# Scores of an attention kernel: six half-row matmuls per head pair become four full-row matmuls over stacked high and low parts

## The reference

```python
xn = layernorm(x)
q  = heads(cq @ Wu_q) + heads(rope(cq @ Wq_r))      # cq  = xn @ Wd_q
k  = heads(ckv @ Wu_k) + heads(rope(xn @ Wk_r))     # ckv = xn @ Wd_kv
v  = heads(ckv @ Wu_v)
x  = x + layernorm(softmax(q k^T / sqrt(1040)) v @ Wo)
h  = gelu(layernorm(x) @ W1[7])
x  = x + layernorm((h @ W2[7]) * router_prob[7])
```

## Time and profile before

| | us |
|---|---|
| median of 2 runs (7258.16 to 7260.33) | 7259.24 |
| profiled execution | 7265.72 |
| its span, slowest core | 7264.1 |
| spans of the 8 cores | 7222.0 to 7264.1 |
| TensorE busy | 5700.7 (78%) |
| VectorE busy | 4018.6 (55%) |
| ScalarE busy | 2148.1 (30%) |
| chain of work that ended last, TensorE's share | 73% |

### The profile page before, as it was taken

One profiled execution on the slowest core, in us unless ns is written; L12 is line 12 of the kernel. 1 busy time (PEld: TensorE's weight loads), 2 busy tenths in 40 slices (PEclk: granted clock), 3 DMA queues, 4 the chain that ended last, 5 costly groups with the idle time before them and its releaser, 6 DMA issues.

```text
span 7264.1 us, 94919 instructions; the slowest of 8 cores (7222.0 to 7264.1 us)
## 1 busy us (share of the span) xinstructions
PE 5700.7 (78%) x26128; PEld 2435.2 (34%) x26128; DVE 4018.6 (55%) x7572; ACT 2148.1 (30%) x3157; POOL 189.0 (3%) x446
## 2 busy tenths in 40 slices
PE   3888888858788888888888888884546898888982
PEld 1333333323333333333333333331223343333430
DVE  3444444434388888888888888881223333333323
ACT  1111222111244444444444444442221011110113
POOL 1000000000000000000000000000000000000000
PEclk9888889879889988998898889886767999999996
DMA  4111111131111121111211121112101111111012
GB/s 110 47 47 47 52 52 52 50 80 37 50 50 51 51 59 52 52 51 52 59 51 51 48 64 51 51 48 62 35 32 38 25 28 35 35 35 33 22 34 90
DMA packets 480103, 357.82 MB, mean 49 GB/s; under 512 B 106863, under 2 KB 436591, under 8 KB 479612
## 3 DMA queue, kind: packets, MB, share of 16 engines
q1 hardware_dynamic: 445532, 316.05, 15.1%
q0 software_dynamic: 34080, 35.71, 3.0%
HBM read 294.73 MB, written 75.76 MB: 51 GB/s over the span
## 4 chain that ended last, share of the span: by engine, by line
PE 73%; DVE 11%; DMA 7%; issue 4%; ACT 4%; SPq 1%; DVEq 0%; ACTq 0%; POOL 0%; POOLq 0%
PE pall L288 42%; PE pall L863 18%; PE pall L900 9%; PE pall L905 4%; DVE sq_scr L943 3%; DMA w1h_sb<-w 2%; DMA kt_sb<-kT_hbm 1%; ACT sq_scr L303 1%; ACT sq_scr L300 1%; DVE xnTh_t L446 1%; ACT xn L432 1%; DVE sq_scr L954 0%; DVE ol_t L962 0%; DVEq L88 0%; DVE w1l_sb L1152 0%
## 5 line engine op out<-in xcount | busy, mean ns | idle before, releaser
L921 ACT ACTIVATE pt<-pall,negM 128x512 f32<-128x512 f32 x2048 | 1403.9, 687 | 1473.1 <-DVE ptl L930 687.2
L930 DVE TENSOR_TENSOR ptl<-pt,pth 128x512 bf16<-128x512 f32 x2048 | 1418.4, 693 | 219.4 <-DVE pth L926 8.3
L863 PE MATMUL pall<-pth,vt_sb 128*65 128x512 bf16 x4096 | 1330.4, 387 | 0.0
L926 DVE CAST pth<-pt 128x512 bf16<-128x512 f32 x2048 | 860.7, 420 | 107.1 <-ACT pt L921 98.4
L905 PE MATMUL pall<-qt_sb,kt_sb 64*128 64x512 bf16 x3072 | 857.2, 389 | 2.1 <-ACT pt L921 1.6
L900 PE MATMUL pall<-qt_sb,kt_sb 64*128 64x512 bf16 x3072 | 786.2, 391 | 81.5 <-DMA kt_sb<-kT_hbm 56.9
L863 PE MATMUL pall<-ptl,vt_sb 128*65 128x512 bf16 x2048 | 787.3, 384 | 4.3 <-DVE ptl L930 4.3
L863 PEld LDWEIGHTS pall<-pth,vt_sb 128*65 128x65 bf16 x4096 | 460.2, 112 | 598.6 <-issue 235.1
L288 PE MATMUL pall<-xn2Th_sb,w1h_sb 128*128 128x512 bf16 x1024 | 403.0, 394 | 255.3 <-DVE w1l_sb L1152 255.3
L1206 DVE TENSOR_TENSOR y_acc<-y_acc,pall 128x512 f32<-128x512 f32 x512 | 351.8, 687 | 280.8 <-PE pall L288 275.8
L1236 ACT ACTIVATE ao_t<-pall,b_col 128x512 f32<-128x512 f32 x128 | 88.0, 687 | 1396.4 <-PE pall L288 1270.6
(11 more groups left out here) (235 smaller groups left out, 6531.2 us busy)
## 6 DMA issues: line engine op xcount, KB each, us to landing
vt_sb<-v_hbm SPq DMA_DIRECT2D x512, 130.0 KB, 2.5
kt_sb<-kT_hbm SPq DMA_DIRECT2D x512, 128.0 KB, 2.4
xt<-xv SPq DMA_DIRECT2D x48, 512.0 KB, 4.1
wscr<-w SPq DMA_DIRECT2D x128, 128.0 KB, 2.3
wscr<-w SPq DMA_DIRECT2D x32, 512.0 KB, 4.4
v_hbm<-vh_t SPq DMA_DIRECT2D x32, 260.0 KB, 2.1
v_hbm<-vl_t SPq DMA_DIRECT2D x32, 260.0 KB, 2.1
xnT_hbm<-xnTh_t SPq DMA_DIRECT2D x64, 128.0 KB, 1.9
```

What stands on the lines that cost most here:

```text
L863: e.matmul(PB(hh)[0:65, 0:512], vf(), pf(), start=(kcp == 0 and pi == 0), stop=(kcp == 31 and pi == 2)), deps=dd)
L921: tex = p.do("scalar", lambda e, sbb=sbb, s32=s32: e.activation(pt32[:, 512 * s32:512 * s32 + 512], PB(sbb)[:, 0:512], AF.Exp, bias=negM[: ...
L926: thv = p.do("vector", lambda e, s=s, s32=s32: e.tensor_copy(pth[:, 512 * s:512 * s + 512], pt32[:, 512 * s32:512 * s32 + 512]), deps=[tex ...
L930: tlv = p.do("vector", lambda e, s=s, s32=s32: e.tensor_tensor(ptl[:, 512 * s:512 * s + 512], pt32[:, 512 * s32:512 * s32 + 512], pth[:, 5 ...
```

## The change

The high and low parts of a head are stacked on the partitions, so that one matmul contracts over 128 rows instead of 64. For Q, `qt_sb` holds for each head its high part on partitions 0 to 63 and its low part on 64 to 127. For K, the left half of `kt_sb` has [high; low] and the right half [low; high]. A first matmul gives hh + ll, a second lh + hl: so two full-row matmuls per head in place of three half-row ones, and the product ll is computed as well. `kt_sb` is twice as large, and `kT_hbm` has the layout [128, 32 chunks, 16 heads, 128], with the high part in rows 0 to 63.

```diff
-    kT_hbm = nc.dram_tensor("kT_hbm", [D, S // 128, 2, 128], BF16, kind="Internal").ap()
+    kT_hbm = nc.dram_tensor("kT_hbm", [128, S // 128, H, 128], BF16, kind="Internal").ap()
...
-            t1 = p.do("sync", lambda e, oc=oc, st=st: e.dma_start(
-                out=kT_hbm[128 * oc:128 * oc + 128, 4 * st:4 * st + 4, 0, :],
...
-            tsp = p.do("sync", lambda e, oc=oc, st=st: e.dma_start(
-                out=kT_hbm[128 * oc:128 * oc + 128, 4 * st:4 * st + 4, 1, :],
...
+            tsp = None
+            for ab in range(2):
+                h = 2 * oc + ab
+                t1 = p.do("sync", lambda e, h=h, ab=ab, oc=oc, st=st, tsp=tsp: e.dma_start(
+                    out=kT_hbm[0:64, 4 * st:4 * st + 4, h, :],
...
+                    deps=[th_, tl_] + ([tsp] if tsp is not None else []),
+                    dma=f"osp{oc}")
+                tsp = p.do("sync", lambda e, h=h, ab=ab, oc=oc, st=st, t1=t1: e.dma_start(
+                    out=kT_hbm[64:128, 4 * st:4 * st + 4, h, :],
...
+                    deps=[th_, tl_, t1], dma=f"osp{oc}")
...
-    kt_sb = [bsb(f"kt_sb{i}", [128, 512], BF16) for i in range(2)]
+    kt_sb = [bsb(f"kt_sb{i}", [128, 2 * 512], BF16) for i in range(2)]
...
-                qload.append(p.do("sync", lambda e, Q=Q, hp=hp, hl=hl: e.dma_start(
-                    out=qt_sb[:, 2048 * (2 * hp + hl):2048 * (2 * hp + hl) + 2048],
...
+        for h in range(4):
+            tqh = p.do("sync", lambda e, Q=Q, h=h: e.dma_start(
+                out=qt_sb[0:64, 2048 * h:2048 * h + 2048],
...
+            qload.append(p.do("sync", lambda e, Q=Q, h=h: e.dma_start(
+                out=qt_sb[64:128, 2048 * h:2048 * h + 2048],
...
+                deps=[LU.get("qt_sb"), tqh], dma=f"qld{h}"))
...
+                tk0 = p.do("sync", lambda e, Q=Q, kc=kc, bufi=bufi: e.dma_start(
+                    out=kt_sb[bufi][:, 0:512].rearrange("p (h k) -> p h k", k=128),
+                    in_=kT_hbm[:, kc, 4 * Q:4 * Q + 4, :]),
+                    deps=[LU.get(("kt", bufi))], dma=f"kt{bufi}")
+                tk1 = p.do("sync", lambda e, Q=Q, kc=kc, bufi=bufi: e.dma_start(
+                    out=kt_sb[bufi][0:64, 512:1024].rearrange("p (h k) -> p h k", k=128),
+                    in_=kT_hbm[64:128, kc, 4 * Q:4 * Q + 4, :]),
+                    deps=[LU.get(("kt", bufi)), tk0], dma=f"kt{bufi}")
                 tk = p.do("sync", lambda e, Q=Q, kc=kc, bufi=bufi: e.dma_start(
-                    out=kt_sb[bufi][:].rearrange("p (a hl k) -> p a hl k", a=2, k=128),
-                    in_=kT_hbm[256 * Q:256 * Q + 256, kc, :, :]
-                        .rearrange("(a p) hl k -> p a hl k", p=128)),
-                    deps=[LU.get(("kt", bufi))], dma=f"kt{bufi}")
+                    out=kt_sb[bufi][64:128, 512:1024].rearrange("p (h k) -> p h k", k=128),
+                    in_=kT_hbm[0:64, kc, 4 * Q:4 * Q + 4, :]),
+                    deps=[LU.get(("kt", bufi)), tk1], dma=f"kt{bufi}")
...
+                for hh in range(4):
+                    sb = 4 + hh
...
+                    t1 = p.do("tensor", lambda e, k1=k1, qs=qs, sb=sb: e.matmul(
+                        PB(sb)[:, 0:512], k1(), qs(), start=True, stop=False),
+                        deps=deps_s + bk.pre_write(sb))
+                    t2 = p.do("tensor", lambda e, k2=k2, qs=qs, sb=sb: e.matmul(
+                        PB(sb)[:, 0:512], k2(), qs(), start=False, stop=True),
+                        deps=deps_s)
```

More of the change, by code:

```diff
@@ L836, in build_program @@
         qload = []
-        for hp in range(2):
-            for hl in range(2):
-                qload.append(p.do("sync", lambda e, Q=Q, hp=hp, hl=hl: e.dma_start(
-                    out=qt_sb[:, 2048 * (2 * hp + hl):2048 * (2 * hp + hl) + 2048],
-                    in_=qT_hbm[256 * Q + 128 * hp:256 * Q + 128 * hp + 128, hl, :]),
-                    deps=[LU.get("qt_sb")], dma=f"qld{2 * hp + hl}"))
+        for h in range(4):
+            tqh = p.do("sync", lambda e, Q=Q, h=h: e.dma_start(
+                out=qt_sb[0:64, 2048 * h:2048 * h + 2048],
+                in_=qT_hbm[256 * Q + 64 * h:256 * Q + 64 * h + 64, 0, :]),
+                deps=[LU.get("qt_sb")], dma=f"qld{h}")
+            qload.append(p.do("sync", lambda e, Q=Q, h=h: e.dma_start(
+                out=qt_sb[64:128, 2048 * h:2048 * h + 2048],
+                in_=qT_hbm[256 * Q + 64 * h:256 * Q + 64 * h + 64, 1, :]),
+                deps=[LU.get("qt_sb"), tqh], dma=f"qld{h}"))
         for qt in range(4):
@@ L886, in build_program @@
                 sc_tok = [None] * 4
[L887 to L903, removed]
-                    for pi, (kf, qf) in enumerate([(kh, qh), (kh, ql), (kl, qh)]):
-                        tB = p.do("tensor", lambda e, kf=kf, qf=qf, sb1=sb1, pi=pi: e.matmul(
-                            PB(sb1)[:, 0:512], kf()[64:128, :], qf()[64:128, :],
-                            start=(pi == 0), stop=(pi == 2), tile_position=(64, 0)),
-                            deps=deps_s + (bk.pre_write(sb1) if pi == 0 else []))
-                    bk.wrote(sb0, tA)
-                    bk.wrote(sb1, tB)
-                    sc_tok[2 * hp] = tA
-                    sc_tok[2 * hp + 1] = tB
@@ new lines, in build_program @@
+                deps_s = [tk] + qload
+                for hh in range(4):
+                    sb = 4 + hh
+                    k1 = lambda bufi=bufi, hh=hh: kt_sb[bufi][:, 128 * hh:128 * hh + 128]
+                    k2 = lambda bufi=bufi, hh=hh: kt_sb[bufi][:, 512 + 128 * hh:
+                                                              512 + 128 * hh + 128]
+                    qs = lambda hh=hh, qt=qt: qt_sb[:, 2048 * hh + 512 * qt:
+                                                    2048 * hh + 512 * qt + 512]
+                    t1 = p.do("tensor", lambda e, k1=k1, qs=qs, sb=sb: e.matmul(
[4 more added lines that the diff above has]
+                        deps=deps_s)
+                    bk.wrote(sb, t2)
+                    sc_tok[hh] = t2
```

10 lines of the change are left out of this document (4 added, 6 removed).

## The result

The changed kernel is slower. The ratio of its time to that of the kernel before is 1.1923 (95% interval 1.1905 to 1.194), which on 7259.24 is 8655 us. The executions behind it lie between 8638.65 and 8663.67 us, and those of before between 7254.73 and 7260.33. In some executions of either kernel the cores of one die run at a lower granted clock and the time is some per cent longer (with them the median of all 11 is 8874.75), and comparisons here leave these out. The profiled execution took 8659.47.

A forecast was written before the change was run, and what follows sets the result against it. VectorE was taken to set the pace at 4.53 us per chunk, TensorE close behind. K loads 854, K stores 145 and Q loads 42 sum to 1041 us, added to 7259 for 8300; range 7950 to 8720.

The forecast's parts named there:

- upper bound of 7.1: Attention stage: us per chunk with all high bounds taken together; 6.4 was expected and 5.8 the low end.
- signs named ahead: Profile after: V issues 6 to 6.7 us apart, SP's K waits some 1600 us, VectorE idle up some 850, clock near 1.00.
- VectorE sets the pace before: Attention stage, kernel before: casts and subtractions fill 4.45 of 4.53 us per chunk; K load has about 1.3 us of slack.
- Score matmuls a draw: Attention scores: eight full-row matmuls need 8 slots, as now; gain 0, bounds a 0.45 us loss and 0.9 gain per chunk.
- K loads, 854 us: Attention stage: three chained loads make chunks 6.4 us for 4.56, over 464 intervals; bounds 575 and 1180.
- first term: Two-chunk loop: start of scores(k-1) to issue of V(k), 4.67 us, with TensorE's work unchanged.
- Rival A: Attention stage: TensorE's clock falls and half of the chunks run at the low level; 8900 us, chance 0.05.
- 0.66 for late landings: Two-chunk loop: 0.22 us added for each of three landings, as not all are at the median; 0.33 per chunk.
- K stores, 145 us: First stage: four stores with three waits per 128 columns delay V stores; 8 tiles x 18 us, bounds 88 and 225.
- Q loads, 42 us: Start of each of four head groups: eight loads with four waits, 11 us later each; bounds 25 and 60.
- Rival B: K loads: rows 128 KB apart in HBM make each landing 3.0 us; 7.7 per chunk, 8960 us, chance 0.10.
- Rival C: Whole kernel: waits are hidden, landings of 1.15 us each, VectorE still sets 4.53; 7260 us, chance 0.03.

The follow-up runs named there:

- the last pair: Changed kernel without SP's waits and kernel before, both with two casts on ScalarE and K ahead of V: ratios to kernel before 0.984 and 0.9868.
- e6_before_chain: Kernel before with its K load cut into three DMAs, each waiting for the landing of the one before: 8237.13 us, 6.66 per chunk.

## Why the prediction was right or wrong

The forecast was 8300 us, 1041 over before, in a range of 7950 to 8720; by the ratio it is 8655, 1396 over. The direction, the place and the mechanism of the waits are borne out. What is missing is the clock that falls in their idle time, and the size is 355 us short. That 8655 still lies in the range is luck: the chunks' 7.03 us is just under the upper bound of 7.1, which was built from slow and late landings, and the landings were neither; the clock filled that room. Of the signs named ahead, the K load as what TensorE waits for, the scores' 1.8 us and VectorE's busy time held. V issues came 7.03 us apart for 6 to 6.7, SP's waits were 1852 us for 1600, VectorE's idle time rose by 1161 for 850, the x loads went 26 us later for 18, and the granted clock in a block was 0.86 to 0.90 for 1.00.

- VectorE sets the pace before, with the K load 1.3 us from binding: right (casts moved: 4.56 to 4.41 per chunk; K load behind four issues: it binds).
- Score matmuls a draw: right, by the last pair: 1.76 us for eight full rows, 1.65 for twelve half ones. The Trainium skill (TensorEngine Tiling (Array Packing), Theoretical Speedup) gives up to 2x for a contraction of at most 64 rows, which for twelve half-row matmuls is six slots, an estimate of 1.3 us at 0.22; the trace agrees in the direction, and shows about 1.6x in this run (1.65 us) and 1.4x in the kernel before (1.82).
- K loads, 854 us: measured 1146. The step that failed is its first term, "start of scores(k-1) to issue of V(k) ... 4.67 ... TensorE's work is unchanged". The work is unchanged, the clock isn't: from 3827.19 to 3833.43 it took 6.24. Rival A was set aside because "the new gaps are short". The mean gap of 1.9 us was right (1.83), but once the clock had fallen it came as 3.4 in one chunk of two. I had the clock as a rival apart, with a chance of 0.05 and the price of half of all chunks; it was a part of the likeliest case, at 385 us. (The Trainium skill, TensorE: Matmul & The Clock Gate, HAM oscillation, describes a loop in which TensorE waits for a DMA in each turn, falls to the low clock in the wait and starts each turn at it. The forecast didn't weigh that section. The trace agrees in that the clock falls once per loop behind the long wait, 0.86 to 0.90 inside the blocks; it differs in that the first matmuls after the wait still have slots of 0.22 us.) The other terms were good: landings of 2.28, 2.15 and 2.13 for 2.4, 2.0 and 2.0, and 0.35. The 0.66 for late landings in a loop was too much: at a full clock the loops came to 12.4 on the mean, for 12.75. That error hid some of the first.
- K stores, 145 us: measured 220, within the bounds of 88 to 225. The mis-sized terms are the wait and the last issue (7.5 us per `oc` for 6.8: three distances of 2.2 to 2.4 for 2.1, and 0.73 for 0.5) and the low clock behind VectorE's wait of 29.36 us: 0.50 for 7 us, where 253 to 260 in the kernel before had 1.00.
- Q loads, 42 us: too low. SP waited 3.4 to 4.9 us from a pair's first load to its second, where I had 3.0 and an issue, and from the first Q load to the scores the second group took 28.9 for 9.9, 19 us where I had 11. The four groups lost 15.2, 19.0, 15.3 and 16.1, 66 in all, just above the bound of 60. Chunks and Q loads together are 1212, and the stage lost 1197; the rest of it gave 15 back.
- Rival B, long landings by the 128 KB stride: fell. The new layout gave 2.4 us for 128 KB and 2.1 for 64 KB, the old one 2.4 and, in `e6_before_chain`, 2.2. The Trainium skill (DMA: Bandwidth & Descriptors, Anatomy of one DMA) fits 2.0 us and bytes over 436e3 for GpSimd's path, which is an estimate of 2.3 and 2.15; the trace agrees for SP's queue to 0.1. Rival C, waits hidden: fell with it.

## What to carry to other kernels

When a transfer is cut into pieces, put the wait for them on the engine that uses the data, with a semaphore for each piece; a wait on the issuing queue adds one landing (2.0 to 2.4 us here for 32 to 128 KB) and delays all that stands behind it. Then look at what stands behind: with double buffers the loop can close through another engine, and moving one load ahead of another was worth 505 us with every wait in place. And don't price TensorE's idle time by its mean alone: here 1.8 us per chunk on the mean began as 1.6 in each, and once one wait had cost TensorE its clock, the slow chunk took up the next wait and made the one after it 3.4, which cost the clock again.

## What the runs showed of the hardware

- A kernel got 380 us faster by more work: 3.4 us of idle time once per loop left a granted clock of 0.86 to 0.90 inside the blocks, and 1.3 us of filler per chunk brought it to 1.00. The fall isn't at the wait: in the loops shown two or three matmuls at the full clock follow it, then some 3.3 us at the low one.
- The size of a load hardly matters at this scale: 32, 64 and 128 KB landed in 2.0, 2.1 and 2.4 us (medians in the chains); 256 KB took 3.7, and 5.7 with eight in flight.
- SP's issue of one DMA takes 0.44 to 0.60 us when queued behind others, so four DMAs per chunk are 2 us of SP's time, which puts the last K load 1.7 us behind V's issue, for 0.57 before.
- Matmuls of 64 rows on the two halves of the array start 0.01 us apart and run side by side even when written in groups of three.
